# Attention A: rotary sines read from PSUM, halves exchanged by transfers, the mix copied by ScalarE and scaled on GpSimd

## What is computed

```python
q = x @ q_a_w.T @ q_b_w.T                      # 16 heads, 64 plain columns + 64 rotated ones
k_pass, v from k_pass_c @ kv_b_w.T             # k_rot is shared by all heads
q_rot: out = [x0 * cos - x1 * sin, x1 * cos + x0 * sin]
scores = einsum('bhqd,bhkd->bhqk', query, key)
attn = softmax(scores)
out = einsum('bhqk,bhkd->bhqd', attn, v) ... @ o_w.T
```

## Time and profile before

| | |
|---|---|
| median of 3 runs | 1534.94 us (1534.45 to 1535.3) |
| the profiled execution's own time | 1532.65 us |
| its span | 1530.8 us |
| mean granted clock of PE | 0.988 |
| busy: PE, DVE, ACT, POOL | 95%, 77%, 55%, 40% |
| opening, attention A | 0 to 53.8 us, 53.8 to 395 us |
| experts, attention B, experts | 395 to 677, to 1246.5, to 1530.8 us |

### The profile page before, as it was taken

The page is one execution under the profiler, slowest core; times in us unless marked ns, Lnnn a source line. Parts: engine busy times, 40 slices in busy tenths (PEclk is TensorE's granted clock), DMA queues, the critical chain, the costliest instruction groups (busy, mean ns, idle before and its releaser), DMA issues. The chain is left out here.

```text
span 1530.8 us, 26737 instructions
## 1 busy us (share of the span) xinstructions
PE 1460.8 (95%) x8904; PEld 1262.2 (82%) x8904; DVE 1171.8 (77%) x2661; ACT 835.6 (55%) x2040; POOL 612.7 (40%) x484
## 2 busy tenths in 40 slices
PE   8799999997899999988999999999999879999998
PEld 6677777776788888876899999999999868888887
DVE  7899999998765555587888888888888777555554
ACT  4788888885433333227766666666666433333322
POOL 2587777874100000017766656666666210000000
PEclk9899999999999999999999999999999999999999
DMA  2265555555210000003223223213222200010001
GB/s 101 55 162 145 148 148 149 155 129 141 84 42 21 22 21 0 1 4 98 52 70 69 63 63 69 70 43 86 67 49 52 53 22 22 21 42 21 0 0 56
DMA packets 73156, 100.17 MB, mean 65 GB/s; under 512 B 10304, under 2 KB 63552, under 8 KB 73024
## 3 DMA queue, kind: packets, MB, share of 16 engines
q1 hardware_dynamic: 73024, 98.55, 24.5%
HBM read 37.56 MB, written 2.23 MB: 26 GB/s over the span
## 5 line engine op out<-in xcount | busy, mean ns | idle before, releaser
L1840 DVE TENSOR_TENSOR f_hidden<-ps,f_silu 128x512 f32<-128x512 f32 x128 | 87.7, 690 | 201.5 <-PE ps L122 201.5
L482 POOL TENSOR_TENSOR ab_swapped<-ab_swapped,const 128x512 f32<-128x512 f32 x126 | 162.9, 1293 | 166.9 <-ACT ab_swapped L477 166.1
L1731 ACT ACTIVATE f_silu<-ps 128x512 f32<-128x512 f32 x128 | 76.3, 598 | 276.2 <-PE ps L122 276.2
L120 PE MATMUL ps<-xh,f_wl 128*128 128x512 f32 x512 | 203.2, 397 | 1.6 <-DVE f_hidden L1840 1.6
L121 PE MATMUL ps<-xl,f_wh 128*128 128x512 f32 x512 | 202.8, 396 | 0.0
L122 PE MATMUL ps<-xh,f_wh 128*128 128x512 f32 x512 | 202.5, 396 | 0.0
L1543 POOL TENSOR_TENSOR ab_qk<-ab_qk,ab_swapped 128x512 f32<-128x512 f32 x126 | 172.5, 1369 | 9.9
L1311 ACT ACTIVATE ab_probs<-ab_probs,ab_negmax 128x128 f32<-128x128 f32 (+1 forms) x256 | 114.6, 449 | 81.9 <-DVE ab_negmax L1414 77.5
L73 POOL TENSOR_TENSOR rstd<-shifted,minus_half 128x4 f32<-128x4 f32 x16 | 16.2, 1013 | 339.6 <-DVE shifted L67 339.6
L120 PE MATMUL ps<-f_wh,f_hl 128*128 128x256 f32 x512 | 144.2, 282 | 0.4 <-DVE x L1856 0.4
L121 PE MATMUL ps<-f_wl,f_hh 128*128 128x256 f32 x512 | 143.9, 281 | 0.0
(11 more groups left out here) (210 smaller groups left out, 4377.8 us busy)
## 6 DMA issues: line engine op xcount, KB each, us to landing
ab_probsT<-ab_squares SPq DMA_DIRECT2D x128, 192.0 KB, 3.6
aa_probsT<-f_stages SPq DMA_DIRECT2D x128, 128.0 KB, 2.6
b_stages<-keys SPq DMA_DIRECT2D x128, 128.0 KB, 2.8
f_stages<-wf_in SPq DMA_DIRECT2D x16, 768.0 KB, 4.4
aa_spread<-inv_rows SPq DMA_DIRECT2D x64, 128.0 KB, 3.0
b_stages<-wb_qkv_in SPq DMA_DIRECT2D x8, 768.0 KB, 6.4
a_stage<-wa_in SPq DMA_DIRECT2D x8, 608.0 KB, 4.3
x<-x_in SPq DMA_DIRECT2D x4, 512.0 KB, 7.2
```

The costliest lines, as they stand in the source:

```text
L120: nc.tensor.matmul(out, ll, rh, start=start, stop=False)
L482: return engine.tensor_tensor(by_batch(out), by_batch(src), table(c, rows, col), ALU.mult)
L1840: nc.vector.tensor_tensor(hidden[:, m, :], UP(m), silu[:, m, :], ALU.mult).then_inc(hid_done, 1)
```

## The change

1. In `rope` for slots from 3 on, DVE multiplies the second half of the PSUM bank by the sines straight away, into rows 0 to 63 of `swapped`. `sines(n+3, 1)` on DVE, the sine product on POOL and the two copies on ACT (`swap`) are gone for these slots.
2. SP exchanges the halves: `move_sines`, two transfers of 32x512 for each head, four per slot, behind `load_spread`. POOL's rotation waits for them (`swap_in`) and subtracts.
3. `normalise` moves from DVE to POOL: ACT copies MIX to `mixed` (`take_mix`, j = 3), POOL multiplies in place. `mixed_hi` moves from j = 0 to j = 1. On POOL one rotation now stands ahead of `mixed_lo`.
4. Folds: keys weights come zero-padded, so two matmuls over 128 rows replace four over 64; ACT and DVE take both heads in one instruction. `fold_output` moves one step later.
5. The five stages share one block: the engines no longer meet between them; a few waits take the place of that.

```diff
@@ fold_product
-    r = slice(64 * h, 64 * h + 64)
     for m in range(2):
-        ins = nc.tensor.matmul(bank[:, m * KVR:(m + 1) * KVR], stage[r, ...], stage[r, A_K:A_K + KVR], start=True, stop=True)
+        ins = nc.tensor.matmul(bank[:, m * P:(m + 1) * P], stage[:, ...], stage[:, A_K:A_K + 2 * KVR], start=True, stop=True)
@@ attention_a, sync
+            def move_sines(n, h):
+                sp.wait_ge(rope_read, 2 * n + h + 1)
+                for to, source in ((64, 32), (96, 0)):
+                    sp.dma_start(swapped[to:to + 32, h, :], swapped[source:source + 32, h, :]).then_inc(swap_in[h], 16)
             for n in range(SLOTS):
                 move_squares(n, 0)
                 if n >= 1:
                     load_spread(n - 1)
+                if 3 <= n + 2 < SLOTS:
+                    move_sines(n + 2, 0)
+                    move_sines(n + 2, 1)
                 move_squares(n, 1)
                 store_inverse(n)
@@ tensor: mix
-                    after(pe, mixed_done, n)
+                    after(pe, mix_read, n)
@@ scalar
+            def take_mix(n):
+                act.wait_ge(pv_done, 2 * n + 2)
+                after(act, mix_lo, n)
+                nc.scalar.copy(mixed[:], MIX).then_inc(mix_read, 1)
-                if j == 0 and n >= 1:
+                if j == 1 and n >= 1:
                     mixed_hi(n - 1)
-                if j < 2 and n + 3 < SLOTS:
-                    swap(n + 3, j)
+                if j == 3:
+                    take_mix(n)
@@ vector
-                times_table(nc.vector, c, raw_of(n, h), first_bank(n, h), ALL_ROWS, C_COSA).then_inc(rope_read, 1)
+                ins = times_table(nc.vector, c, raw_of(n, h), first_bank(n, h), ALL_ROWS, C_COSA)
+                if n >= 3:
+                    ins = times_table(nc.vector, c, swapped[0:64, h, :], first_bank(n, h)[64:128], ROT_ROWS, C_SINA)
+                ins.then_inc(rope_read, 1)
-                if j == 0 and n >= 1:
-                    normalise(n - 1)
-                if j == 2 and n + 3 < SLOTS:
-                    sines(n + 3, 1)
@@ gpsimd: rotate
                 else:
-                    pool.wait_ge(swap_done, 2 * n + h + 1)
-                    times_table(nc.gpsimd, c, other, other, ROT_ROWS, C_SINA).then_inc(side_done, 1)
-                    pool.wait_ge(side_done, n - 2)
+                    pool.wait_ge(swap_in[h], 32 * (n - 2))
                 pool.wait_ge(rope_read, 2 * n + h + 1)
-                nc.gpsimd.tensor_tensor(rows, rows, other, ALU.add).then_inc(rotated, 1)
+                nc.gpsimd.tensor_tensor(rows, rows, other, ALU.add if n < 3 else ALU.subtract).then_inc(rotated, 1)
@@ gpsimd: normalise and the loop
+            def normalise(n):
+                pool.wait_ge(mix_read, n + 1)
+                pool.wait_ge(spread_in[n % 2], 32 * (n // 2 + 1))
+                nc.gpsimd.tensor_tensor(mixed[:], mixed[:], spread[:, n % 2, :], ALU.mult).then_inc(mixed_done, 1)
+                pool.wait_ge(mixed_done, n + 1)
             for n in range(SLOTS):
                 if n >= 1:
+                    normalise(n - 1)
+                if n + 3 < SLOTS:
+                    rotate(n + 3, 0)
+                if n >= 1:
                     mixed_lo(n - 1)
                 if n + 3 < SLOTS:
-                    for h in range(2):
-                        rotate(n + 3, h)
+                    rotate(n + 3, 1)
                     for h in range(2):
                         queries_lo(n + 3, h)
```

More of the change, by code:

```diff
@@ L122, in matmul3, with opening @@
     return nc.tensor.matmul(out, lh, rh, start=False, stop=stop)
-def opening(nc, c, name, a, x, const, small, temperature, order, weights, stage, stage_in):
+def opening(nc, c, block, name, a, x, const, small, temperature, order, weights, stage, stage_in):
     with ExitStack() as ctx:
@@ L513, in fold_output_product, with attention_a @@
     return ins
-def attention_a(nc, c, name, a, weights, stage, stage_in, norm, ahead):
+def attention_a(nc, c, block, name, a, weights, stage, stage_in, norm, ahead):
     SQ, LEAD, SLOTS = 32, 6, HP * NG
@@ L617, in _ @@
             fetch(sp, ahead)
+            sp.wait_ge(pv_done, 2 * SLOTS)
         @block.tensor
@@ L742, in fold_query @@
             def fold_query(it):
[L744 to L747, removed]
+                act.wait_ge(fold_ready, it)
+                fold_upper(nc, FOLD(it)[:, 0:2 * P], stage, wh[:, it % 2]).then_inc(fold_hi, 1)
             def fold_output(it, bank):
@@ L892, in step @@
                     fold_query(fold_after(n))
-                if j == 2 and s == 1 and not last:
+                if j == 3 and s == 1 and not last:
                     fold_output(it + 1, FOLDS)
@@ L1012, in _ @@
                     fold_rest_parts(fold_after(n))
+            normalise(SLOTS - 1)
             mixed_lo(SLOTS - 1)
@@ L1056, in first_projections_b, with attention_b @@
         ins.then_inc(b.proj_ready, 1)
-def attention_b(nc, c, name, b, w_qkv, w_out, stage, wo_stage, stage_in, wo_in, own_norm, norm, ahead):
+def attention_b(nc, c, block, name, b, w_qkv, w_out, stage, wo_stage, stage_in, wo_in, own_norm, norm, ahead):
     W, SQ, LEAD = T + P, 32, 7
@@ L1548, in _, with experts @@
                 norm_rstd(nc, c, norm, pool, s)
-def experts(nc, c, name, weights, stage, stage_in, own_norm, ahead=(), norm=None, result=None, b=None):
+def experts(nc, c, block, name, weights, stage, stage_in, own_norm, ahead=(), norm=None, result=None, b=None):
     with ExitStack() as ctx:
@@ L1959, in hybrid_kernel @@
             a.swap_done, a.sin_done, a.rotated, a.q_hi, a.q_lo = sem("swap_done"), sem("sin_done"), sem("rotated"), sem("q_hi"), sem("q_lo")
+            a.first_fold_lo = sem("first_fold_lo")
             a.inv_rows = nc.dram_tensor("inv_rows", (2, 2 * TG, P), F32, kind="Internal").ap()
             a.squares, a.probsT = [f_stages[:, 0:2 * PAIRS * T], a.keys[:]], b_stages[:]
-            opening(nc, c, "open", a, x, const, small, temperature, order, wa, a_stage, a_in)
-            attention_a(nc, c, "aa", a, wa, a_stage, a_in, norm2, [(f_stage[:, e], wf[e], f1_in[e]) for e in range(2)])
+            opening(nc, c, block, "open", a, x, const, small, temperature, order, wa, a_stage, a_in)
+            attention_a(nc, c, block, "aa", a, wa, a_stage, a_in, norm2, [(f_stage[:, e], wf[e], f1_in[e]) for e in range(2)])
         with ExitStack() as inner:
@@ L1970, in hybrid_kernel @@
             b.stage, b.wo_stage, b.stage_in, b.wo_in = b_stage, bo_stage, b_in, bo_in
[L1971 to L1973 removed]
+            experts(nc, c, block, "f1", wf, f_stage, f1_in, norm2, ahead=[(b_stage[:], wb_qkv[0], b_in), (bo_stage[:], wb_out[0], bo_in)], norm=norm3, b=b)
+            attention_b(nc, c, block, "ab", b, wb_qkv, wb_out, b_stage, bo_stage, b_in, bo_in, norm3, norm4, [(f_stage[:, e], wf[e], f2_in[e]) for e in range(2)])
+        experts(nc, c, block, "f2", wf, f_stage, f2_in, norm4, result=(out.rearrange("(t p) d -> p t d", p=P), stored))
 def constants():
@@ L2025 @@
     kvb = w["L0_attn_a_kv_b_w"].reshape(HP, 2, NOPE + VD, KVR)
-    wk = kvb[:, :, :NOPE].reshape(HP, P, KVR)
+    wk = _np.zeros((HP, 2, NOPE, 2, KVR), _np.float32)
+    for h in range(2):
+        wk[:, h, :, h, :] = kvb[:, h, :NOPE]
+    wk = wk.reshape(HP, P, 2 * KVR)
     wv = kvb[:, :, NOPE:].transpose(0, 2, 1, 3).reshape(HP, P, 2 * KVR)
```

88 lines of the change are left out of this document (35 added, 53 removed).

## The result

| | before | after |
|---|---|---|
| median | 1534.89 us (4 runs, 1534.45 to 1535.3) | 1640.82 us (4 runs, 1637.99 to 1643.06) |
| ratio, 95% interval | | 1.069 [1.0668, 1.0711] |
| span of the profiled execution | 1530.8 us | 1639.1 us |
| mean granted clock of PE | 0.988 | 0.957 |

The account below looks back on a forecast made before the run. DVE was taken to bound the kernel before, a loop through the exchange and POOL's rotation after: 28 slots from 10.0 to 13.6 us, +100.8, less 3 elsewhere, +98 on 1532.65; forecast 1632 us, range 1595 to 1673.

Parts of the forecast that it names:

- The loop through POOL's rotation: Attention A: row maximum, squares, spread, exchange, POOL's rotation and low part, PE's output, next row maximum; 13.6 us a slot.
- Its length up to PE's output: Attention A slot, from row maximum to POOL's low part done, for which PE's output waits: 11.18 us.
- R: The instant of a slot's row maximum of step j = 0 on DVE, from which the loop's times count.
- The last leg: PE's output to next row maximum: 0.72 us output at full clock plus 1.66 us scores at half clock.
- my end of 14.3 us a slot: Attention A with every PE burst after the wait starting at half clock: 14.3 us a slot, 1652 us.
- The number of equal slots: Attention A: 28 slots each lengthened from 10.0 to 13.6 us, +100.8 us.
- the loop holds for n = 1 to 28: Attention A: slots whose POOL iteration has both a mix and a rotation take 13.6 us, 28 of them.
- What lies in the air: DVE, ACT and POOL work during PE's wait: DVE's savings, fold waits, take_mix and mixed_hi change nothing in the time.
- Outside the slots: Last three slots -1 us, stage boundaries and earlier ACT work -2 us: -3 us together.
- The exchange is hidden: Rival, attention A: halves land by R + 4.9, slots of about 9.5 us, 1518 us; chance 6%.
- SP's queue is the bound: Rival, attention A: rotations in time, SP's four more issues make 10.2 us a slot, 1538 us; chance 3%.
- The clock stays low: Rival, PE in attention A: clock does not recover within a slot, up to 17 us each, 1728 us; chance 5%.

Follow-up runs that it names:

- e2: The changed kernel with SP issuing the exchange (move_sines) ahead of load_spread: 1599.25 us, 1.0421 of the kernel before.
- e10: The changed kernel with SP's exchange issued ahead of the first squares, both heads in one transfer: 1670.66 us, 1.0893 of the kernel before.
- e1: The changed kernel with mixed_lo ahead of both rotations in POOL's queue: 1589.19 us, 1.0359 of the kernel before.
- e3: The changed kernel with normalise back on DVE, mixed_hi back at j = 0 and POOL's earlier order: 1584.88 us, 1.0336 of the kernel before.
- e4: The changed kernel with the rotary part of before (no exchange by transfers), normalise still on POOL: 1550.89 us, 1.012 of the kernel before.
- e5: The changed kernel with rotary part and normalisation as before, keeping 128-row folds, later output fold and one block: 1523.3 us, 0.9943 of the kernel before.
- e7: The changed kernel with the exchange issued from ACT's queue in place of SP's: 1580.89 us, 1.0317 of the kernel before.

## Why the prediction was right, and where its sizes were off

The mechanism, the sign and the size held; the steps by themselves:

- **The loop through POOL's rotation** held: e2 shortened it by about its spread's issue time, e10 lengthened it, e1 and e3 cut PE out of it and took 52 to 56 us.
- **Its length up to PE's output** was forecast as R + 11.18; the mean over the 27 slots is R + 11.19. That it fits so well is luck: an issue takes 0.62 us (2.49 / 4), not 0.45, while the first exchange leaves at R + 5.29, not 5.38, and head 0's second transfer lands after a median of 2.49 us, not 2.6. The Trainium skill, SBUF — State Buffer, section "The DMA setup-cost knee", gave an estimate of 2.15 us for 64 KB. The measurement lies between that and my row, and decides.
- **The last leg** was forecast as 2.38 us, output at full and scores at half clock. It measured 2.57 on average, and the middle is hardly ever met: 18 of 27 legs are at half clock practically throughout (2.78 to 2.97), six at full (1.73), three in between. This is the mis-sized term of the steady slot: 13.76 in place of 13.6, 4.4 us over 27 slots. The Trainium skill, TensorE: Matmul & The Clock Gate, section "HAM oscillation", describes a loop in which each burst after a transfer wait starts low. The trace agrees for 18 bursts of 27 and not for the others. All of them low was my end of 14.3 us a slot; 13.76 lies nearer to my 13.6.
- **The number of equal slots** was wrong by one. I gave the first of the 28 the price of the others, +3.6; it cost +9.1, through ACT. The term "the loop holds for n = 1 to 28" missed that before the first mix another wait takes the loop's place. These 5.5 us, the 4.4 above and 0.5 outside the slots are the whole gap between the forecast +98 and the +108.3 us of the span (1632 and 1640.8 in medians).
- **What lies in the air** held while the loop ran: the saving on DVE brought nothing. But "take_mix and mixed_hi also lie in that air" was true only because of the loop. With the loop gone the move to POOL costs 28 us (e4 against e5), which no step of mine names; and the folds' 4.8 us come back.
- **Outside the slots**: -3 forecast, -2.5 measured. The sine product takes 0.693 us (0.69 forecast), and DVE's busy share in the stretch is 70% as forecast.
- **"The exchange is hidden"** fell at the place named: it needed halves at R + 4.9, and even when ACT issues them at once, in e7, they land at R + 6.9 on average. **"SP's queue is the bound"** fell: SP stands idle between the inverse rows and the next squares. **"The clock stays low"** fell: PE recovers within the slot, 0.87 on average. (Its price was also added up wrongly: twice 9.5 us is 19, not 17.) The loss was a wait, with some 15 us of clock in it. PE's own wait before the output was forecast as 4 us or so and is 3.1.

## What to carry to other kernels

Before putting a transfer into a per-slot chain, add up the loop it closes: issue position, every issue ahead of it in that queue, landing, and what stands behind the waiting instruction on its engine. If that is longer than the slot, the saving on the bound engine is worth nothing. An order that helps one consumer can starve another (PE's low part, ACT's queries), so after a reordering read the waits again before expecting the whole loss back. And take a losing change apart: 10 us of gain lay in this one (e5), under 116 of loss.

## What the runs showed of the hardware

- PE's clock after a wait went two ways: in the changed kernel the legs after waits of 2.93 us or more were at half clock, but for one after 3.20 us that began at full, and those after 2.00 to 2.83 us began at full. With ten matmuls of no use in the wait, 22 of 27 legs had the short form in place of 7, and the kernel took 15 us less.
- A filler matmul of 128x128 in float32 took 0.23 us (5.96 / 26) and shows as two records (x52 for 26).
- The same form of transfer landed in 2.4 us from SP's queue in the changed kernel and in 2.8 us from ACT's in e7, with other transfers beside it (64 KB, medians of 68 and 77). Of the four that SP issues in a row, the first two landed after 2.6 and 2.5 us, the last two after 2.1 and 2.0 (medians); one of 128 KB in e10 took 2.4 us from SP, so twice the size cost nothing that the medians show.
